# Issuing the operand loads of a 12-head attention one per key step instead of nine to sixteen at a time

## The reference

```python
attn = jnp.einsum('bqc,bkc->bqk', q * scale, k)           # 12 heads of 16 channels
rel_h = jnp.einsum('bhwc,hkc->bhwk', r_q, Rh)
rel_w = jnp.einsum('bhwc,wkc->bhwk', r_q, Rw)
attn = (attn.reshape(B * nh, H, W, H, W) + rel_h[:, :, :, :, None] + rel_w[:, :, :, None, :]).reshape(B * nh, H * W, H * W)
attn = jax.nn.softmax(attn, axis=-1)
out = jnp.einsum('bqk,bkc->bqc', attn, v)
```

## Time and profile before

| | us |
|---|---|
| median of 3 runs (lowest, highest) | 1222.81 (1218.33, 1223.66) |
| the profiled execution's own time | 1223.77 |
| its span, first to last instruction | 1221.6 |
| PE busy | 1048.2 (86%) |
| DVE busy | 859.6 (70%) |
| ACT busy | 706.2 (58%) |
| mean granted clock of PE | 0.910 |

### The profile page before, as it was taken

How to read it: one execution, slowest core, us unless ns; L and a number is a source line. 1 busy time by engine, 2 the same in 40 slices (tenths; PEclk the granted TensorE clock), 3 DMA queues, 4 the chain that set the end, 5 groups by cost and what they waited for, 6 DMA issues and landing times.

```text
span 1221.6 us, 35977 instructions
## 1 busy us (share of the span) xinstructions
PE 1048.2 (86%) x15434; PEld 742.3 (61%) x15434; DVE 859.6 (70%) x1702; ACT 706.2 (58%) x1008; POOL 190.2 (16%) x159
## 2 busy tenths in 40 slices
PE   4867679999989999999999998999898884793997
PEld 2545135666767666666777665677465763671776
DVE  3737768898979988998889997899237664132442
ACT  3556047676757776776767776777754341231554
POOL 2530027000000000000000000000246552000443
PEclk9885579999989999999999999999998886795999
DMA  7598796655736573747464655556100100221111
GB/s 113 146 222 261 186 185 109 102 93 94 123 62 99 88 123 62 121 74 114 72 113 79 107 92 93 78 89 99 36 1 21 39 10 13 60 58 33 30 40 30
DMA packets 83338, 109.13 MB, mean 89 GB/s; under 512 B 14349, under 2 KB 75569, under 8 KB 82996
## 3 DMA queue, kind: packets, MB, share of 16 engines
q1 hardware_dynamic: 82660, 105.17, 45.7%
q10 hardware_dynamic: 528, 1.77, 1.1%
HBM read 85.47 MB, written 21.44 MB: 88 GB/s over the span
## 4 chain that ended last, share of the span: by engine, by line
PE 68%; issue 9%; DVE 8%; DMA 6%; POOL 4%; ACT 3%; SPq 1%; ACTq 1%; POOLq 0%; DVEq 0%
PE ps L1020 35%; PE ps L1171 17%; PE ps L1015 14%; DVE mx_p L1461 3%; DVE xh L104 2%; POOL hid L742 2%; DVE stage_lo L1433 1%; DMA mask<-in_c_mask 1%; DMA rel_d<-stage_lo 1%; POOL rstd L112 1%; ACT hid L937 1%; ACT hid_f L943 1%; DMA m_d<-mneg 1%; PE ps L1120 1%; POOL x L756 1%
## 5 line engine op out<-in xcount | busy, mean ns | idle before, releaser
L1461 DVE TENSOR_REDUCE mx_p<-ps 128x1 f32<-128x464 f32 (+1 forms) x1080 | 611.6, 629 | 81.7 <-PE ps L1020 72.1
L890 ACT ACTIVATE prob<-ps 128x768 f32<-128x768 f32 x648 | 497.2, 810 | 246.3 <-PE ps L1020 245.6
L1020 PE MATMUL ps<-kc,qc 112*32 112x464 f16 (+1 forms) x4320 | 482.0, 375 | 20.0 <-DMA qc<-rel_d 11.0
L1020 PE MATMUL ps<-qv,ka 113*32 113x384 f16 x5184 | 424.5, 333 | 35.3 <-issue 25.3
L1171 PE MATMUL ps<-prob,v_ext 128*32 128x384 f32 x2592 | 310.3, 497 | 9.4 <-issue 9.4
L1020 PEld LDWEIGHTS ps<-qv,ka 113*32 113x32 f16 x5184 | 226.2, 99 | 118.5 <-issue 58.3
L1020 PEld LDWEIGHTS ps<-kc,qc 112*32 112x32 f16 x4320 | 187.1, 97 | 115.5 <-issue 35.0
L1171 PEld LDWEIGHTS ps<-prob,v_ext 128*32 128x32 f32 x2592 | 121.8, 112 | 31.9 <-issue 15.5
L715 POOL COPY v_ext<-v_all 128x288 f32<-128x288 f32 x12 | 5.1, 428 | 561.7 <-PE ps L1171 561.7
L1015 PE MATMUL ps<-w_dn,hid 128*96 128x192 f16 x864 | 83.9, 262 | 7.7 <-ACT hid L937 7.7
L1015 PEld LDWEIGHTS ps<-w_dn,hid 128*96 128x96 f16 x864 | 81.2, 134 | 14.3 <-ACT hid L937 8.8
(11 more groups left out here) (104 smaller groups left out, 859.1 us busy)
## 6 DMA issues: line engine op xcount, KB each, us to landing
qv<-rel_d SPq DMA_DIRECT2D x216, 144.0 KB
qv<-kq_d SPq DMA_DIRECT2D x108, 216.0 KB
qc<-rel_d SPq DMA_DIRECT2D x24, 216.0 KB, 4.2
xin<-in_x SPq DMA_DIRECT2D x12, 288.0 KB, 3.5
kq_d<-khl SPq DMA_DIRECT2D x24, 144.0 KB, 2.2
q_h<-kq_d SPq DMA_DIRECT2D x9, 288.0 KB, 4.8
q_w<-qw_d SPq DMA_DIRECT2D x9, 288.0 KB, 7.2
rel_d<-stage_hi SPq DMA_DIRECT2D x4, 648.0 KB, 8.0
```

The lines of the kernel that those rows point to most:

```text
L890: nc.scalar.activation(prob[:, s4(p, s), :].rearrange("p (a b) -> p a b", a=2), ps[:, 3 + 2 * (s % 2):5 + 2 * (s % 2), 0:CW], ACT.Exp).the ...
L1020: ins = nc.tensor.matmul(ps[c:c + 32, bank, 0:w], l[:, c:c + 32], r, start=True, stop=True, tile_position=(0, c))
L1461: nc.vector.tensor_reduce(mx_p[:, q * GT + k // MP, k % MP:k % MP + 1], ps[:, slot, 0:min(MW, N - k % MP * MW)], AX, ALU.max).then_inc(uni ...
```

## The change

Each DMA of a load gets a wait of its own on `s_ps`. The nine of `load_qv` are issued at steps 0 to 8 of a group, one a step. The three of `load_k` go behind `m_through_dram` and wait for steps 13 to 15. The four of `load_c` go into the period's second group, behind its `m_through_dram`, and wait for steps 13 to 16 of it (steps 31 to 34 of the head). Sizes, buffers and semaphores stay as they are; the very first loads (`load_k(0, 0)`, `load_qv(0, 0, 0)`, `load_c(0, 0)`, `load_c(1, 1)`) pass no step and are issued as before.

```diff
+        M_STEP = 13
...
-            def load_c(n, p):
+            def load_c(n, p, step=None):
...
-                for dst, src in parts:
+                for i, (dst, src) in enumerate(parts):
+                    if step is not None:
+                        sp.wait_ge(s_ps, step + i)
                     sp.dma_start(dst, src.rearrange("o p t -> (o p) t")).then_inc(c_in[p], 16)
...
-            def load_k(n, p):
+            def load_k(n, p, step=None):
                 for r, part in enumerate((0, 0, 1)):
+                    if step is not None:
+                        sp.wait_ge(s_ps, step + r)
...
-            def load_qv(n, q, b):
+            def load_qv(n, q, b, step=None):
...
-                for dst, src in parts:
+                for i, (dst, src) in enumerate(parts):
+                    if step is not None:
+                        wait_used(sp, s_ps, step + i)
                     sp.dma_start(dst, src).then_inc(qv_in[b], 16)
...
                 for q in range(1, NQ):
-                    wait_used(sp, s_ps, n * STEPS + (q - 1) * GS)
-                    load_qv(n, q, (p + q) % 2)
+                    step = n * STEPS + (q - 1) * GS
+                    load_qv(n, q, (p + q) % 2, step)
+                    m_through_dram(n, p, q, units_to(n, "mt", q))
                     if q == 1 and not last:
-                        load_k(n + 1, 1 - p)
-                    m_through_dram(n, p, q, units_to(n, "mt", q))
+                        load_k(n + 1, 1 - p, step + M_STEP)
+                    if q == 2 and not last and not is_at(n, NH - 2):
+                        load_c(n + 2, p, step + M_STEP)
...
-                if not is_at(n, NH - 2):
-                    load_c(n + 2, p)
-                sp.wait_ge(s_ps, n * STEPS + (NQ - 1) * GS)
-                load_qv(n + 1, 0, 1 - p)
+                load_qv(n + 1, 0, 1 - p, n * STEPS + (NQ - 1) * GS)
                 m_through_dram(n + 1, 1 - p, 0, units_to(n, "mt", NQ))
```

## The result

The changed kernel takes 1163.6 us in the median of 4 runs (1161.3 to 1172.8) against 1223.2 for the kernel before (1218.3 to 1227.6); the ratio is 0.954 with a 95% interval of 0.950 to 0.958. Three more series, on chips 3 and 13, held the kernel before beside the experiments; in one of them the changed kernel, unedited, was timed again (0.955, 0.952 to 0.958). The forecast was 1174 with a range of 1158 to 1216: the direction, the place and the mechanism hold, the gain was 60 us where I had summed 49.

What follows compares the result with a forecast made beforehand. PE was taken to be bounding, with attention stops from late instruction packets behind SP's load queue. Stops 35.7 and clock 13.3 us, together 49.0, off 1223.8 give 1174.8, stated as 1174 for the median; range 1158 to 1216.

Steps and rivals of the forecast that it cites:

- No load was late; the stops were the loss: Attention, 199 to 862 us: PE hardly waits for data; its 39.7 us of unexplained waits in 25 stops are the loss.
- The stops are late instruction packets: PE in the attention runs out of instructions because q8's packet comes only when SP's queue of loads is worked off.
- the undisturbed pace: Attention without stops: 18.16 us a group, 40.4 PE instructions a us, so a q8 packet due every 6.3 us.
- slack: How late a q8 packet may be without stopping PE: 3.7 us, taken from two stops.
- One sign of the prediction: In the changed kernel's trace q8's packets would come some 6.3 us apart, never over 10.
- The backlog by arithmetic: SP's load queue ahead of a packet: about 5.6 us before, at most 3.3 after; 4.0 us of stops remain.
- The clock: PE's granted clock, 0.98 over the attention's 663 us, returns to full speed: 13.3 us won (9.9 to 16.6).
- The sum: Whole kernel: 35.7 us of stops and 13.3 of clock, together 49.0 us won.
- Waits, maxima, heads 0 and 1: SP's added waits cost 0; maxima stay on time with 2.7 us to spare; no gain or loss before 199 us.
- The slower rival: The attention's maxima come late behind the spread loads, PE stands 2.1 us in each of 33 groups: 1244 us; chance 0.10.
- Partial: Rival: each of the attention's 25 stops stays with 1 us, the clock returns; 28 us won, 1195 us; chance 0.18.
- no change: Rival: the depth of SP's queue q1 is not what holds q8 back; 1223 us (1216 to 1230); chance 0.12.

Runs made afterwards that it cites:

- Nine at once: Changed kernel with the nine loads of a group issued together at its first step, the added waits kept: 1211.1 us, 0.995 of the kernel before.
- six and three: Changed kernel with six of the nine loads issued together at step 0 and three at step 6: 0.973 of the kernel before.
- Every second step: Changed kernel with the nine loads issued at steps 0, 2, ... 16 of a group: 1244.8 us, 1.021 of the kernel before.
- three at a time: Changed kernel with the nine loads issued in threes at steps 0, 3 and 6: 1167.2 us, 0.959 of the kernel before.

## Why the prediction was right

**No load was late; the stops were the loss.** Right. In all these kernels PE's work in the attention is the same, and the time follows the stops and the waits for the maxima.

**The stops are late instruction packets.** Nine at once brought them back, six and three gave half of them, three and one hardly any. The prediction inferred from two stops that PE had run out of instructions; a count over the instruction records of the traces shows it. Take the instructions that PE has started when a stop ends, matmuls, weight loads and its own waits, and subtract 256 for each q8 packet that had started by then, the last one left out. At every stop in the stretches read here, 106 in the traces of all kernels, what remains is 449 or 450; PE's 33 waits for the maxima in *Every second step* give anything from 196 to 452. So PE always stops at the same place of a block of 256 instructions, and goes on 2.5 to 3.6 us after the next packet has started. From one packet to the next it takes 256 instructions in the mean, in the kernel before and in the changed one, so q8 is PE's queue. (The one wait of 1.6 us for ACT leaves 450 as well and belongs to these stops.)

Where the changed kernel has its one stop above 1 us, these are its queues in 532.8:533, 533:543.7 and 543.7:543.9, and the row of the chain.

```profile
q8 instruction: 1, 0.02, 39.2%
...
q1 hardware_dynamic: 713, 1.31, 78.9%
...
q8 instruction: 1, 0.02, 53.1%
```

```profile
545.44 1.60 issue
```

The packet started 10.9 us after the last, 4.6 later than the 6.3 of the undisturbed pace, and PE stopped for 1.6 us: a slack of 3.0. I had 3.7 from two stops; the 18 stops of the kernel before that follow a gap of over 10 us give 2.6 to 4.0. One sign of the prediction failed: no gap between packets was to be over 10 us, and the changed kernel has six, of 10.1 to 10.9 us, each with a stop (the kernel before has 19, up to 13.6).

**The backlog by arithmetic.** Right in order, rough in size, and in part lucky. 5.2 us of stops remained where 4.0 were forecast, but not for the reason given. I had let a tenth remain because 3.3 us, the top that the nine alone make, is so near the slack. In fact all six stops stand where other transfers went right ahead of the nine, `load_c`'s four in three of them, `load_k`'s three in one, the filters' in two; behind the nine alone no gap between packets is over 9.4 us. For three at a time the same arithmetic gave 8 to 12 us of stops and there were 6.2.

That depth sets the lateness can be read from the traces. I call a packet due when the count above stands at 184, the least at which one started; PE then has 265 instructions left, 6.6 us at 40.4 a us. The backlog is what SP has handed over and the DMA engines have not yet moved at that moment. From 280 us to the last write of the maxima, the mean delay in us from due to start (number of packets):

| backlog, MB | kernel before | nine at once | six and three | changed kernel |
|---|---|---|---|---|
| under 0.1 | 1.4 (28) | 1.4 (29) | 0.9 (27) | 0.7 (29) |
| 0.3 to 0.5 | 2.9 (12) | 2.4 (7) | 2.2 (12) | 2.4 (28) |
| 0.5 to 0.7 | 3.2 (10) | 3.0 (12) | 3.4 (24) | 3.3 (6) |
| 0.7 and more | 5.1 (25) | 5.0 (24) | 5.3 (7) | none |

At one backlog the delay is about the same in all four; the kernels differ in how often a packet meets a deep one. The due time is inferred, so the delays are estimates.

**The clock.** I took 13.3 us from a clock of 0.98 and let all of it come back; the clock is 1.00 in the changed kernel. By the trace's clock records 30.7 us of the 663 stood at 0.50, so the term should have been 15.4, within the bounds that I gave. The clock fell after stops, but not in step with the idle time: 0.99 with 32.2 us of stops, 1.00 with 16.7 and less, and 0.99 with the 69.2 us of waits of *Every second step*, which come in pieces of 2.1 us and were followed by 0.50 only twice.

**The sum was 11 us short.** Between first and last write of the maxima 56.0 us were won (662.9 - 606.9). Stops give 34.5 of it (39.7 - 5.2; I had 35.7), waits for data 1.5 (3.1 - 1.6) and the clock at most 15.4. The other 4.6 us or more I had counted at nothing: of the 63.6 us above the undisturbed pace only 53.0 were stops and clock as read, and I let the remaining 10.6 stand. By the earlier trace rows and the row of the changed kernel above, PE's busy time fell by 19.0 us for the same matmuls (620.15 to 601.13), more than the clock explains; a slower start after each stop would do that, but no run separates it. The pace of 18.16 us, taken 33 times, was the better estimate, and it stands in the prediction only as the low end. The remaining 3.1 us of the span's 59.1 lie ahead of 199 us (1.2) and behind the last maxima (1.9), where one execution of each says little.

**Waits, maxima, heads 0 and 1.** Right: the waits cost nothing visible, and the maxima were on time (1.6 us of waits for `qv<-m_d`, 1.5 before). But the room that I gave them was wrong. In the kernel before the write goes out 13.1 us after the group's first score (427.44 to 440.54 us), not 11.6, and between the issue of the read-back at 441.72 and the next group's first score at 445.60 lie 3.9 us, of which the read-back takes 2.7: 1.2 us are to spare, not 2.7. The slower rival's 2.1 us a group, which *Every second step* then measured, agrees by chance: there the write went out 15.8 us after the first score and took 2 us instead of 1.2.

**Partial and no change.** The partial rival had 1 us left in each of 25 stops; it was 5.2 us in 6. A q8 packet is neither free of q1's backlog (12.0 us without one in the kernel before) nor bound to wait for q1's end: in the changed kernel one starts at 361.29 us, with the queue full from 356 to 363 us. The Trainium skill's "DMA: Bandwidth & Descriptors", section "Queues, rings and completion order", has the engines take turns between queues packet by packet; the doses of one, three, six and nine do not agree with it as far as instruction packets beside a deep queue go: by taking turns the delay would not grow with the backlog, and it does, from about 1 to 5 us. Why it does, no run here shows.

## What to carry to other kernels

Where an engine with a long written-out program stands still and its wait has no releaser, look at when the packets of the instruction queue came and at what the data queue had been handed shortly before. Hand over transfers at the pace at which they are moved, small pieces between large ones, even if the data is needed much later; keep the sum well ahead of its deadline, and put short chains that the engines do wait for in front of the bulk. A wait on a step spreads nothing if the issuing queue reaches it after the step has passed: check the times of issue, not the program.

## What was not expected of the hardware

- A stop can cost more than itself: after 3.67 us the granted clock was 0.63 over 4 us, after 3.40 us it was 0.50 over 332 to 334 us. It need not: with nine at once a stop of 2.66 us at 565.44 us, with six and three one of 2.73 at 553.22, left it at 1.00. No stop for instructions of 1.9 us or less in the stretches read here was followed by 0.50.
- The instruction packets can be some 3 to 4 us late at 40.4 instructions a us. They take 1.1% of the DMA engines' time, and their lateness was most of the 4.6% that the change won.
- The section on the kernel speaks of heads 2 to 9 as passes of a loop. That is a loop of the program that writes the instructions (L608 of the kernel before, a plain `range`); on the engines the heads lie one behind the other, and PE takes a new packet for every 256 instructions all along.
